# Local attention's projections in three float32r passes, with split weights kept in DRAM

## The reference

```
DEPTH, HEADS, DIM_HEAD, WINDOW = 6, 16, 64, 32      # INNER = 1024
def attn_layer(x, Wqkv, qs, ksc, Wo):
    qkv = x @ Wqkv                                  # (2, 1024, 128) @ (128, 3072)
    q, k, v = jnp.split(qkv, 3, -1)
    ...
    q = l2norm(q) * qs
    k = l2norm(k) * ksc
    q = q * cos * scale + rotate_half(q) * sin * scale
    k = k * cos * inv + rotate_half(k) * sin * inv
    out = local_attention(q, k, v)
    return out.transpose(0, 2, 1, 3).reshape(b, n, INNER) @ Wo
```

## Time and profile before

| | us |
|---|---|
| time, median of 3 runs | 4008.13 (4006.91 to 4010.7) |
| the profiled execution | 3999.94 |
| its span | 3998.2 |
| PE busy | 3499.2 (88%) |
| DVE busy | 2983.8 (75%) |
| ACT busy | 2425.5 (61%) |
| POOL busy | 1393.6 (35%) |

### The profile page before, as it was taken

How to read it: one execution, slowest core, us unless ns; L and a number is a source line. 1 busy time by engine, 2 the same in 40 slices (tenths; PEclk the granted TensorE clock), 3 DMA queues, 4 the chain that set the end, 5 groups by cost and what they waited for, 6 DMA issues and landing times. The chain is left out here.

```text
span 3998.2 us, 103162 instructions
## 1 busy us (share of the span) xinstructions
PE 3499.2 (88%) x41084; PEld 2106.6 (53%) x41125; DVE 2983.8 (75%) x5780; ACT 2425.5 (61%) x4554; POOL 1393.6 (35%) x634
## 2 busy tenths in 40 slices
PE   7979678888849958999999999999999986998898
PEld 3347433333327735666666666666666663222665
DVE  5958757777739867777778777778778855887685
ACT  3336437777728826676666676676676652555472
POOL 3720011111100007676666675666666630000000
PEclk8979859999969979999999999999999996999899
DMA  1000047777602002322322322322322211100000
GB/s 40 0 6 6 11 161 231 232 232 231 196 12 69 11 0 64 98 61 56 99 60 59 97 59 58 99 57 62 97 58 63 58 42 59 35 25 13 14 15 11
DMA packets 174521, 285.75 MB, mean 71 GB/s; under 512 B 36819, under 2 KB 76628, under 8 KB 172116
## 3 DMA queue, kind: packets, MB, share of 16 engines
q1 hardware_dynamic: 173460, 278.40, 23.8%
q10 hardware_dynamic: 576, 0.69, 0.0%
HBM read 103.97 MB, written 74.45 MB: 45 GB/s over the span
## 5 line engine op out<-in xcount | busy, mean ns | idle before, releaser
L2298 POOL TENSOR_TENSOR b2f_norm<-b2f_norm,b2f_minus_half 128x16 f32<-128x16 f32 x192 | 555.1, 2909 | 275.5 <-DVE b2f_norm L2639 275.5
L2288 POOL TENSOR_TENSOR b2f_q<-b2f_q,b2f_q_part 128x1024 f32<-128x1024 f32 x96 | 228.1, 2376 | 693.7 <-DVE b2f_q_part L2629 693.7
L1720 ACT ACTIVATE b1a_weights<-b1a_b_ps 128x512 f32<-128x512 f32 x512 | 277.2, 596 | 39.4 <-PE b1a_b_ps L1645 37.2
L1835 DVE TENSOR_REDUCE b1a_tops<-b1a_a_ps 128x1 f32<-128x512 f32 (+3 forms) x512 | 244.6, 502 | 19.5 <-PE b1a_a_ps L1601 17.9
L2581 ACT ACTIVATE b2f_v_rows<-b2f_q_ps 128x1024 f32<-128x1024 f32 x96 | 98.3, 1024 | 262.6 <-PE b2f_q_ps L2360 153.5
L1552 POOL TENSOR_SCALAR b1a_k_op<-b1a_k_op,b1a_extra 128x1024 bf16<-128x1024 bf16 x32 | 90.7, 2845 | 446.5 <-DMA b1a_k_op<-part_copies 409.3
L1720 ACT ACTIVATE b3a_weights<-b3a_b_ps 128x512 f32<-128x512 f32 (+3 forms) x384 | 161.2, 502 | 136.8 <-PE b3a_b_ps L1655 135.6
L2638 DVE TENSOR_REDUCE b2f_norm<-xn 128x16 f32<-128x1024 f32 x192 | 234.2, 1220 | 12.0 <-ACT xn L2522 4.8
L2531 ACT ACTIVATE b2f_prob<-b2f_odd_ps,b2f_bias,b2f_norm 128x64 f32<-128x64 f32 x768 | 232.6, 447 | 6.2 <-DVE b2f_bias L2655 4.9
L2531 ACT ACTIVATE b2f_prob<-b2f_even_ps,b2f_bias,b2f_norm 128x64 f32<-128x64 f32 x768 | 232.6, 451 | 2.3 <-DVE b2f_bias L2655 2.3
L2291 POOL TENSOR_TENSOR b2f_k<-b2f_k,b2f_k_part 128x1024 f32<-128x1024 f32 x96 | 227.2, 2367 | 0.7 <-DVE b2f_k_part L2629 0.7
(11 more groups left out here) (528 smaller groups left out, 9301.7 us busy)
## 6 DMA issues: line engine op xcount, KB each, us to landing
b2f_values<-b2f_v_rows SPq DMA_DIRECT2D x1534, 64.0 KB
position_scratch<-b1a_e_sb SPq DMA_DIRECT2D x128, 512.0 KB, 4.0
b1a_band<-position_scratch SPq DMA_DIRECT2D x128, 384.0 KB
b2f_wqkv<-in_b2f_wqkv SPq DMA_DIRECT2D x6, 1536.0 KB, 7.3
b2f_turn<-in_c_rotary SPq DMA_DIRECT2D x6, 1024.0 KB, 8.6
b1f_raw<-in_b1f_both SPq DMA_DIRECT2D x9, 512.0 KB, 3.7
part_copies<-b1a_parts SPq DMA_DIRECT2D x12, 256.0 KB
b2f_wo<-in_b2f_wo SPq DMA_DIRECT2D x6, 512.0 KB, 9.8
```

The costliest lines, as they stand in the source:

```text
L1720: act.activation(weights[:, s % P_RING, c, lo:QW], b_room(s, c)[:, lo:QW], ACT.Exp).then_inc(S.exps_ready, 1)
L1835: ins = dve.tensor_reduce(out, src, AX_X, ALU.max)
L2288: pool.tensor_tensor(G.q[:, g % 2], G.q[:, g % 2], G.q_part[:], ALU.add) \
L2298: pool.tensor_tensor(part, part, G.minus_half[:, 0:HEADS], ALU.pow) \
```

## The change

Each projection becomes three float32r passes into the same place in PSUM: input head with weight head, input tail with weight head, input head with weight tail. A head is a float32 number copied to float32r, a tail is what is left.

- The weights of all six layers are split ahead, in 12 halves of 128x1536, in block 1's attention: SP loads a half, POOL copies its head and subtracts for its tail after a group's key variants, and SP stores both in DRAM (`wqkv_parts`). This stands in SP's stream at the fifth step of each of the first 12 groups.
- On chip there is room for one layer's parts. The first layer's are fetched in block 1's feed-forward; the later ones at a layer's last tile, queries' and keys' columns after that tile's query and key projection, values' columns after its 16 moves.
- A tile's input is split by POOL at the end of its step for the tile before (`split_tile(s + 1)`), into a ring of four. PE's projection waits for it (`x_tailed`).

```diff
-              wqkv=two("wqkv", 3 * INNER), wo=two("wo", PAIRS, P), w1=two("w1", 6, P), w2=two("w2", 3, P),
+              wqkv=M.sb("b2f_wqkv", [P, 2, 3 * INNER], F32R), wo=two("wo", PAIRS, P), w1=two("w1", 6, P), w2=two("w2", 3, P),
...
+def projection_weights(K, w, l, lo, hi):
+
+    return [(w.wqkv[:, part, lo:hi].bitcast(F32), K.wqkv_parts[l, part, :, lo:hi]) for part in range(2)]
...
                             pool.tensor_scalar(k_op[:, g % K_RING, kind], k_op[:, g % K_RING, 0],
                                                extra[:, 1 + kind:2 + kind], None, ALU.add) \
                                 .then_inc(S.k_kinds, 1)
+                        if g < 2 * LAYERS:
+                            pool.wait_ge(S.raw_loaded, 16 * (g + 1))
+                            if g:
+                                pool.wait_ge(S.raw_stored, 32 * g)
+                            pool.tensor_copy(raw_parts.head[:], raw[:]).then_inc(S.raw_headed, 1)
+                            pool.wait_ge(S.raw_headed, g + 1)
+                            pool.tensor_tensor(raw_parts.tail[:], raw[:], raw_parts.head[:].bitcast(F32),
+                                               ALU.subtract).then_inc(S.raw_tailed, 1)
...
+                    def load_half(n):
+                        if n:
+                            sp.wait_ge(S.raw_tailed, n)
+                        sp.dma_start(raw[:], to_split[n // 2, :, cols(n % 2, half_wide)]) \
+                            .then_inc(S.raw_loaded, 16)
+
+                    def store_half(n):
+                        sp.wait_ge(S.raw_tailed, n + 1)
+                        for part, tile in enumerate((raw_parts.head, raw_parts.tail)):
+                            sp.dma_start(K.wqkv_parts[n // 2, part, :, cols(n % 2, half_wide)],
+                                         tile[:].bitcast(F32)) \
+                                .then_inc(S.raw_stored, 16)
+
+                    load_half(0)
                     for t in range(STEPS + 1):
+                        if t % QT == 4 and t // QT < 2 * LAYERS:
+                            store_half(t // QT)
+                            if t // QT + 1 < 2 * LAYERS:
+                                load_half(t // QT + 1)
...
+X_RING = 4
...
+            x_parts=M.sb("b2f_x_parts", [P, X_RING, 2, P], F32R),
...
             for g in range(n_tiles):
+                ends = g % TILES == TILES - 1 and layer(g) + 1 < LAYERS
+                if ends:
+                    sp.wait_ge(S.qk_ready, 4 * g + 4)
+                    for dst, src in projection_weights(K, G, layer(g) + 1, 0, 2 * INNER):
+                        sp.dma_start(dst, src).then_inc(S.keys_loaded, 16)
                 sp.wait_ge(S.v_copied, g + 1)
...
+                if ends:
+                    for dst, src in projection_weights(K, G, layer(g) + 1, 2 * INNER, 3 * INNER):
+                        sp.dma_start(dst, src).then_inc(S.values_loaded, 16)
...
+            def split_tile(g):
+
+                l, at = layer(g), at_column(g % TILES)
+                if l:
+                    pool.wait_ge(S.stored, 2 * (g // per_q - QUARTERS + 1))
+                if g >= X_RING:
+                    pool.wait_ge(S.v_ready, g - X_RING + 1)
+                head, tail = (G.x_parts[:, g % X_RING, part] for part in range(2))
+                pool.tensor_copy(head, G.xs[:, at:at + P]).then_inc(S.x_headed, 1)
+                pool.wait_ge(S.x_headed, g + 1)
+                pool.tensor_tensor(tail, G.xs[:, at:at + P], head.bitcast(F32), ALU.subtract) \
+                    .then_inc(S.x_tailed, 1)
+
             pool.wait_ge(S.began, INIT)
+            split_tile(0)
             for s in range(n_steps):
...
                     for piece in range(2):
                         scale_table(layer(s) + 1, 2 * (s % TILES - 12) + piece)
+                if s + 1 < n_tiles:
+                    split_tile(s + 1)
...
-            def tile_input(g):
-                return G.xs[:, at_column(g % TILES):at_column(g % TILES) + P]
+            def project(g, ps, weights):
+                head, tail = (G.x_parts[:, g % X_RING, part] for part in range(2))
+                for n, (a, b) in enumerate(((head, 0), (tail, 0), (head, 1))):
+                    ins = pe.matmul(ps, a, weights(b), start=(n == 0), stop=(n == 2))
+                return ins
...
-                if l and g % per_q == 0:
-                    pe.wait_ge(S.stored, 2 * (g // per_q - QUARTERS + 1))
+                    if l:
+                        pe.wait_ge(S.keys_loaded, 16 * PROJECTION_LOADS * l)
+                pe.wait_ge(S.x_tailed, g + 1)
...
-                    pe.matmul((Z.q, Z.k)[j // 2][:, j % 2], tile_input(g), G.wqkv[:, l % 2, cols(j, QW)],
-                              start=True, stop=True).then_inc(S.qk_ready, 1)
+                    project(g, (Z.q, Z.k)[j // 2][:, j % 2],
+                            lambda part: G.wqkv[:, part, cols(j, QW)]).then_inc(S.qk_ready, 1)
...
+                if g % TILES == 0 and layer(g):
+                    pe.wait_ge(S.values_loaded, 16 * PROJECTION_LOADS * layer(g))
...
-                    ins = pe.matmul(Z.q[:, h], tile_input(g), wv[:, :, h], start=True, stop=True)
+                    ins = project(g, Z.q[:, h], lambda part: wv[:, part, :, h])
...
+                 wqkv_parts=nc.dram_tensor("wqkv_parts", [LAYERS, 2, P, 3 * INNER], F32,
...
-            block1_ffn(nc, K, W, choice, xn, x, fetch)
+            block1_ffn(nc, K, W, choice, xn, x, fetch + projection_weights(K, w, 0, 0, 3 * INNER))
```

More of the change, by code:

```diff
@@ L1052, in layer_weights @@
     return [(dst[:, l % 2], src) for dst, src in
-            ((w.wqkv, of("b2f_wqkv")), (w.turn, W["c_rotary2"]), (w.scales, of("b2f_scales")),
+            ((w.turn, W["c_rotary2"]), (w.scales, of("b2f_scales")),
              (w.wo, of("b2f_wo")), (w.w1, of("b2f_w1")), (w.w2, of("b2f_w2")),
@@ L1241, in head_attention @@
         project_heads(nc, K, W, weights, key, xn, weights.w, small, q_op, k_op, values, relative)
-        attend(nc, K, key, q_op, k_op, extra, ident, values, table, unseen, merged, relative, fetch)
+        attend(nc, K, key, q_op, k_op, extra, ident, values, table, unseen, merged, relative, fetch,
+               W["b2f_wqkv"] if relative else None)
         merge_heads(nc, K, key, merged, x, weights.w, relative)
@@ L1422, in attend @@
 def attend(nc, K, key, q_op, k_op, extra, ident, values, table, unseen, merged, relative,
-           fetch):
+           fetch, to_split):
     kinds = 3 if relative else 1
@@ L1499, in attend @@
             scratch = K.scratch
+            half_wide = 3 * INNER // 2
+            raw = M.sb(f"{key}_raw", [P, half_wide])
+            raw_parts = two_parts(M, f"{key}_raw", [P, half_wide])
         shift_parts = shift_cols[:].rearrange("p t (h c) -> p (t h) c", h=2)[
@@ L1505, in attend @@
                    "turned_scores", "exps_ready", "out_added", "o_copied", "o_turned",
-                   "merged", "fetched", "dve_chain") as (block, S):
+                   "merged", "fetched", "raw_loaded", "raw_headed", "raw_tailed", "raw_stored",
+                   "dve_chain") as (block, S):
             queries, keys = (S.queries_even, S.queries_odd), (S.keys_even, S.keys_odd)
@@ L1786, in _ @@
                             sp.dma_start(band[:, r % BANDS], skewed).then_inc(band_loaded[r % 2], 16)
+                    sp.wait_ge(S.raw_stored, 32 * 2 * LAYERS)
             @block.vector
@@ L2213, in layers_of_attention @@
     n_steps = n_tiles + 2 * per_q
-    LOADS = 7
+    LOADS = 6
+    PROJECTION_LOADS = 2
     def layer(g):
@@ L2237, in layers_of_attention @@
                "spread_ready", "gained", "normed", "g_ready", "gelu_done", "a_ready", "hidden_done", "z_ready",
-               "stored", "x_added", "dve_chain") as (block, S):
+               "stored", "x_added", "x_headed", "x_tailed", "keys_loaded", "values_loaded",
+               "dve_chain") as (block, S):
         weights = (S.weights_even, S.weights_odd)
@@ L2357, in project_v @@
                     pe.wait_ge(S.y_stored, 2 * (g - 2))
-                wv = G.wqkv[:, layer(g) % 2, 2 * INNER:].rearrange("k (p h d) -> k p h d", h=2, d=HD2)
+                if g % TILES == 0 and layer(g):
+                    pe.wait_ge(S.values_loaded, 16 * PROJECTION_LOADS * layer(g))
+                wv = G.wqkv[:, :, 2 * INNER:].rearrange("k n (p h d) -> k n p h d", h=2, d=HD2)
                 for h in range(2):
-                    ins = pe.matmul(Z.q[:, h], tile_input(g), wv[:, :, h], start=True, stop=True)
+                    ins = project(g, Z.q[:, h], lambda part: wv[:, part, :, h])
                 ins.then_inc(S.v_ready, 1)
@@ L2977, in load_constants @@
                  copies=nc.dram_tensor("part_copies", [B, 2, 3, P, T], BF16, kind="Internal").ap(),
+                 wqkv_parts=nc.dram_tensor("wqkv_parts", [LAYERS, 2, P, 3 * INNER], F32,
+                                           kind="Internal").ap(),
                  **tiles)
```

## The result

| | before | after |
|---|---|---|
| time, median (us) | 4007.52 (4006.36 to 4010.7) | 4281.61 (4275.64 to 4293.05) |
| ratio, 95% interval | | 1.0689 (1.0672 to 1.0707) |
| span of the profiled execution | 3998.2 | 4278.4 |
| block 1's attention, from its first position product to block 1's feed-forward | 576.3 | 623.9 |
| from there to block 2's first projection | 357.4 | 366.0 |

The forecast was 4271 us.

The account below looks back on a forecast made before the run. PE was taken to bound block 2 before the change, POOL's split closing a ring after it. 93 (ring) + 122 (clock) + 48 (block 1) = +263 us on the profiled 3999.94, plus 8 to the median: 4271 us, range 4070 to 4395.

Parts of the forecast that it names:

- The ring: Block 2: each split queues behind POOL's previous tile and PE waits; turn 18.3 us, 20.2 with layer norm's root; +93 us.
- One tile in four was to stay with PE: Block 2: the tile from 2453.77 stays bound by PE, loses 1.2 of its 20.55 us and takes 19.3.
- the split's lower bound of 0.55: Block 2: least time for POOL's copy and subtraction with hand-overs, against 0.9 us taken; -0.35 us a tile.
- the low end of the range: Whole kernel: clock holds, split at its lower bound, block 1's transfers hidden; 4068, said as 4070 us.
- The clock: Block 2: PE's idle time lowers its clock, 1.7 us in 72 tiles, +122 us; rival that it holds: 4149 us, chance 0.25.
- so the wait goes: Block 2: DVE's 0.57 us wait for PE's output product vanishes, as that product comes 0.8 us earlier.
- What the change removes: Block 2: cheaper projections on PE save 1.2 us a tile, 115 us over 96 tiles, if PE stays the bound.
- Block 1's attention: Block 1: weight splits hold up SP's queue of position bands, 4.0 us late in twelve halves; +48 us, bounds 0 to +109.
- a late band shifts the rest: Block 1: PE, ACT and DVE take turns in each step, so a band 4.0 us late delays everything behind it.
- the queue: Block 1: SP waits for the split, then issues three 768 KB transfers ahead of the step's write; +48 us.
- The port: Block 2 rival: splits meet DVE's two-SBUF-operand product, half the tiles lose 1.2 us; +58 us, 4329 us, chance 0.14.
- At nothing: Weight fetches, first layer's and next layers', taken as covered and costed at nothing; about 20 us at five layer changes if uncovered.

Follow-up runs that it names:

- lead: Changed kernel, but POOL splits the input two tiles ahead instead of one: 4021.72 us, ratio 1.0061.
- wait alone: Kernel before with its exact float32 products, plus only the input split and PE's wait for it: 4304.91 us, ratio 1.077.
- doubled split: Changed kernel with one more copy and one more subtraction on POOL ahead of each input split: 4365.5 us, ratio 1.091.
- The fill: Changed kernel with ten more float32r passes on PE ahead of its wait, in three tiles of four: 4208.9 us, ratio 1.0537.
- the run with the seventh step: Changed kernel, input split two tiles ahead, weights split before key variants in groups 2 to 13, transfers at a group's seventh step: 4031.68 us, ratio 1.0071.

## Why the prediction was right, and where it was not

- **The ring** came out as worked out: POOL's last instruction is the subtraction, PE starts 0.05 to 0.3 us after it, and in the two full-clock tiles without the root in which POOL's key copy and split met no product of DVE, the split ends 18.4 us after the tile's start, 18.3 in the working (19.4 in the eight others, in which one of them did). The split takes 0.82 us with its gap, 0.9 with the hand-over to PE was taken. Three runs show it as the cause (lead, wait alone, doubled split). Two steps of the working were off without showing in the sum. One tile in four was to stay with PE, and none did: only two of 96 start more than 0.3 us after the split (0.4 and 1.0). And the split's lower bound of 0.55 leaves out the hand-overs that it claims (0.2 + 0.35 + 0.2 is 0.75), so the low end of the range stood some 19 us too low.
- **The clock**: priced at 122 us. In the changed trace lengths are ready 12.75 us after a tile's start in the mean, 11.43 where the clock holds; over 96 tiles that is 127 us. 72 tiles at 1.7 were really 61 at 1.9: a count too high and a price too low that cancel. Not all of the 127 is new, since before 15 tiles of 96 already began slowly. One link was missed: the prediction let DVE's wait for the output product go ("so the wait goes"), and at the full clock 0.26 us of it is left, but with slow passes ahead of that product it is 1.55, beside the 1.3 that the queries come late. The fill shows the idle time as the cause, for at least 72 us of the cost.

DVE at the store of the previous tile, in the tile from 2434.87 and in the slow one from 2454.93:

```profile
2442.97 0.60 DVE L2754 TENSOR_TENSOR b2f_ms<-b2f_xs,b2f_q_ps 64x128 f32<-64x128 f32 x2 [0.26 <-PE b2f_q_ps L2443]
...
2465.84 0.60 DVE L2754 TENSOR_TENSOR b2f_ms<-b2f_xs,b2f_q_ps 64x128 f32<-64x128 f32 x2 [1.55 <-PE b2f_q_ps L2443]
```

- **What the change removes** was over-rated: 0.8 us a tile (78 / 96) instead of 1.2. It did not show, because PE was no bound any more.
- **Block 1's attention**: 48 us forecast, 47.6 found, and the step behind the number was wrong. The prediction said that "a late band shifts the rest" in twelve halves; the runs put 37 us on DVE's product held by POOL's subtraction, with the clock behind it, in ten groups, and some 10 on bands, mostly in the first two groups. The agreement is an accident of two sizes; with the queue's 10 alone the forecast would have been 38 us lower, which is still within its range.
- **The port** was a rival for block 2, where it came to eight splits of 1.7 to 1.9 us in place of 0.8, 8 us and not 58. The rival left out the key copy, which is a link of the ring too: in 18 tiles it met the product and took 0.8 to 1.5 us in place of 0.39, 16 us more in all (before, it did so in 21 tiles, but no projection waited for it). In block 1, where I did not look for it, it decided: there DVE met a POOL instruction of 3.4 us, not one of 0.4. The rule in the Trainium skill ("SBUF — State Buffer", "Who interferes with whom") names this case, a DVE instruction with two SBUF inputs beside a GpSimd one that reads SBUF, and the rows of 782.09 and 784.16 agree with it; the product beside the key variants (last section) does not.
- **At nothing** stood the next layer's weights: 0.3 us of wait in the changed kernel, whose ring covers them, and 21.3 once the ring is open. The cover was named; the price without it (20 us) fits.

## What to carry to other kernels

A producer with plenty of idle time on average can still be the bound if its new work is queued behind everything it does for the tile before: give it a lead in its queue; the ring of four buffers alone did nothing here. Look for long two-operand instructions on POOL beside short ones on DVE's path, in every stage the change touches. And a number that fits is no proof of its mechanism: block 1's fitted to 0.4 us and came from elsewhere.

## What the hardware showed that I had not expected

- In the run with the seventh step, DVE's product took 0.19 us in the midst of POOL's key variants (662.14 to 667.81, one tensor operand in bf16), while beside POOL's float32 subtraction it took up to 3.4. But the second copy behind it took 0.94 us in place of 0.17 and ended 0.03 us after POOL's instruction, and in five groups of that run such a copy ended so. So it depends on both instructions who is held; what decides it, no run here shows. The two timelines:

```profile
666.61 0.19 DVE L1888 TENSOR_TENSOR b1a_tops<-b1a_tops,b1a_band 128x32 f32<-128x32 f32 x1
...
666.90 0.94 DVE L1892 COPY b1a_shift<-b1a_band 128x16 f32<-128x16 f32 x1
```

```profile
662.14 5.67 POOL L1571 TENSOR_SCALAR b1a_k_op<-b1a_k_op,b1a_extra 128x1024 bf16<-128x1024 bf16 x2 [3.28 <-DMA b1a_k_op<-part_copies]
```

- The copy of 128x1536 on POOL took 1.46 us and the subtraction 3.44, where the working had bounds of 2.3 and 3.6.
- The granted clock fell around idle times of 1.8 us (block 1) and 2.9 us (block 2), for 3.41 and 6.83 us.
